# Gated cross-attention block on one core: the pass over the low probabilities last in its unit, auxiliary units in six places instead of three

## What is computed

```python
x = x + tanh(g_xattn[0]) * xattn(layernorm(x), ctx_768, w_q, w_k, w_v, w_o, b_o)
x = x + tanh(g_ffn[0]) * ffn(layernorm(x), ...)

def xattn(x, context, w_q, w_k, w_v, w_o, b_o):        # B=16, Sq=100, Skv=1444
    q, k, v = heads(x @ w_q), heads(context @ w_k), heads(context @ w_v)   # 16 x 64
    attn = softmax(einsum('bhid,bhjd->bhij', q, k) * 64 ** -0.5)
    return merge(einsum('bhij,bhjd->bhid', attn, v)) @ w_o + b_o

def ffn(X, ...):                                        # width 128, 16 heads of 8
    h = rmsnorm(X, norm1_w)
    X = X + self_attention(h @ wq, h @ wk, h @ wv) @ wo
    h2 = rmsnorm(X, norm2_w)
    ...
    return X + shared_swiglu(h2) + top2_experts(h2)
```

## Time and profile before

| | before |
|---|---|
| median of 3 runs | 1532.89 us (1532.3 to 1535.36) |
| the profiled execution | 1536.03 us, span 1534.3 us |
| PE / DVE / ACT / POOL busy | 1374.3 / 1060.1 / 810.3 / 580.3 us |
| mean granted clock of TensorE | 0.965 |
| end of the last score step | about 1365 us; the experts follow |

### The profile page before, as it was taken

One profiled execution on the slowest core, in us unless ns is written; L12 is line 12 of the kernel. 1 busy time (PEld: TensorE's weight loads), 2 busy tenths in 40 slices (PEclk: granted clock), 3 DMA queues, 4 the chain that ended last, 5 costly groups with the idle time before them and its releaser, 6 DMA issues.

```text
span 1534.3 us, 28786 instructions
## 1 busy us (share of the span) xinstructions
PE 1374.3 (90%) x8776; PEld 839.2 (55%) x8776; DVE 1060.1 (69%) x1996; ACT 810.3 (53%) x1188; POOL 580.3 (38%) x702
## 2 busy tenths in 40 slices
PE   4769999999999999999999999899999999888898
PEld 4225555555555565555555555555555555456676
DVE  2777777767676767676767777677767676866665
ACT  1134646555555555555555565556565655554554
POOL 3023334333433434343334333434333433453454
PEclk7579999999999999999999999999999999899999
DMA  7020202020202010010202020202020100000000
GB/s 216 24 56 1 56 1 57 1 58 1 57 1 58 1 32 25 19 39 2 56 2 57 1 57 1 57 1 57 1 58 1 42 1 1 1 1 1 7 7 11
DMA packets 66966, 43.26 MB, mean 28 GB/s; under 512 B 52966, under 2 KB 62410, under 8 KB 66826
## 3 DMA queue, kind: packets, MB, share of 16 engines
q1 hardware_dynamic: 66826, 41.43, 10.7%
HBM read 15.38 MB, written 0.82 MB: 11 GB/s over the span
## 4 chain that ended last, share of the span: by engine, by line
PE 58%; DVE 18%; issue 12%; ACT 4%; POOL 3%; DMA 2%; DVEq 1%; SPq 0%; ACTq 0%; POOLq 0%
PE psum L756 15%; DVE mx L1240 7%; PE psum L816 7%; PE psum L737 6%; PE psum L741 6%; PE psum L739 6%; PE psum L769 4%; PE psum L856 3%; PE psum L808 3%; PE psum L782 3%; PE psum L843 3%; ACT p_hi L952 2%; DVE y_sb L1262 2%; POOL y_sum L575 2%; DVE mx L1274 1%
## 5 line engine op out<-in xcount | busy, mean ns | idle before, releaser
L951 ACT ACTIVATE p<-psum 128x800 f32<-128x800 f32 x384 | 321.1, 836 | 557.2 <-PE psum L741 555.2
L1240 DVE TENSOR_REDUCE mx<-psum 128x1 f32<-128x512 f32 (+1 forms) x624 | 387.6, 654 | 59.2 <-PE psum L816 55.3
L432 POOL TENSOR_TENSOR p_lo<-p,p_hi 128x800 f16<-128x800 f32 x128 | 244.0, 1906 | 482.3 <-ACT p_hi L952 469.3
L756 PE MATMUL psum<-p_hi,c_both 128*128 128x400 f16 x1536 | 390.3, 336 | 26.3 <-POOL p_lo L432 18.0
L952 ACT ACTIVATE p_hi<-psum 128x800 f16<-128x800 f32 x384 | 319.4, 832 | 0.0
L432 DVE TENSOR_TENSOR p_lo<-p,p_hi 128x800 f16<-128x800 f32 x256 | 258.8, 1011 | 54.6 <-issue 20.1
L816 PE MATMUL psum<-cT_both,qk_hi 96*128 96x512 f16 (+1 forms) x624 | 233.2, 388 | 67.3 <-DVE y_sb L1262 19.5
L756 PEld LDWEIGHTS psum<-p_hi,c_both 128*128 128x128 f16 x1536 | 146.7, 98 | 146.0 <-POOL p_lo L432 24.3
L737 PE MATMUL psum<-qk_hi,cT_both 97*128 97x400 f16 x768 | 195.2, 335 | 14.0 <-issue 9.5
L756 PE MATMUL psum<-p_lo,c_both 128*128 128x400 f16 x768 | 194.9, 335 | 0.0
L739 PE MATMUL psum<-qk_lo,cT_both 96*128 96x400 f16 x768 | 194.5, 334 | 0.0
(11 more groups left out here) (183 smaller groups left out, 1774.9 us busy)
## 6 DMA issues: line engine op xcount, KB each, us to landing
c_both<-c_new SPq DMA_DIRECT2D x16, 768.0 KB, 4.0
ctx_nat<-in_ctx_dram SPq DMA_DIRECT2D x16, 528.0 KB
wg<-in_L_ffn_e_gate_dram SPq DMA_DIRECT2D x1, 1024.0 KB, 5.3
wu<-in_L_ffn_e_up_dram SPq DMA_DIRECT2D x1, 1024.0 KB, 7.3
wd<-in_L_ffn_e_down_dram SPq DMA_DIRECT2D x8, 128.0 KB, 4.9
out_dram<-x SPq DMA_DIRECT2D x4, 200.0 KB
x<-in_x_dram SPq DMA_DIRECT2D x1, 600.0 KB
p<-in_L_xattn_w_q_dram SPq DMA_DIRECT2D x1, 512.0 KB, 3.8
```

The source lines that it names most:

```text
L432: engine.tensor_tensor(p_lo[0:m, i % 3, :, :], p32[0:m, i % 3, :, :], p_hi[0:m, i % 3, :, :], ALU.subtract).then_inc(lo_made(b, i)[0], 1)
L756: t = mm(outs[k], w[parity][0:m, j, :], p[0:m, i % 3, k, :], start=(j == 0 and w is c_hi and p is p_hi), stop=(j == CH - 1 and w is c_lo))
L951: a(p32[0:m, i % 3, :, :], src, ACT.Exp, scale=DH ** -0.5)
L1240: v.tensor_reduce(mx[:, rt, part:part + 1], bank[:, 0:w], AX.X, ALU.max)\
```

## The change

In `pv_unit` the pass over `p_lo` moves from second to third place and the wait for it moves in front of that pass. `steps` cuts a step's auxiliary units into sixths, and `score_unit` too now has places for them: behind the first and the second score pass (places 0 and 1), behind the third (2), behind the first and the second value pass (3 and 4), behind the last (5). The cut rounds up: one unit stands in place 0; two in 0 and 3; three in 0, 2 and 4; four in 0, 1, 3 and 4; five in 0 to 4. On DVE, places 0 to 3 come ahead of `p_lo`, 4 and 5 behind. ACT's order is the same as before. A wait for `p_hi` is added before the last two value units, which no score unit precedes.

```diff
-        thirds = [[us[len(us) * k // 3:len(us) * (k + 1) // 3] for k in range(3)] for us in by_place]
-        return thirds, at
+        sixths = [[us[-(-len(us) * k // 6):-(-len(us) * (k + 1) // 6)] for k in range(6)] for us in by_place]
+        return sixths, at
...
-            def score_unit(b, parity, i):
+            def score_unit(b, parity, i, between):
...
                 for k in range(2):
                     mm(outs[k], cT_hi[parity][:, cols], qk_hi[parity][:, qs[k]], start=True, stop=False)
+                between(0)
                 for k in range(2):
                     mm(outs[k], cT_hi[parity][0:C, cols], qk_lo[parity][:, qs[k]], start=False, stop=False)
+                between(1)
                 for k in range(2):
                     t = mm(outs[k], cT_lo[parity][:, cols], qk_hi[parity][0:C, qs[k]], start=False, stop=True)
                 t.then_inc(scores, 1)
...
-                pe.wait_ge(*lo_made(b, i))
                 if i == 0:
                     pe.wait_ge(c_in, (b + 1) * 16)
...
-                for w, p in ((c_hi, p_hi), (c_hi, p_lo), (c_lo, p_hi)):
+                for n, (w, p) in enumerate(((c_hi, p_hi), (c_lo, p_hi), (c_hi, p_lo))):
+                    if p is p_lo:
+                        pe.wait_ge(*lo_made(b, i))
                     for k in range(2):
...
-                    if w is c_hi and p is p_hi:
-                        between()
+                    if n < 2:
+                        between(3 + n)
                 t.then_inc(pv, 1)
...
-                    score_unit(b, parity, i)
-                    one, two, three = steps(kind)[0][i]
-                    run_aux(aux, one, b, kind, parity)
...
+                    score_unit(b, parity, i, between)
+                    between(2)
                     if i >= 2:
-                        pv_unit(b, parity, i - 2, middle)
+                        pv_unit(b, parity, i - 2, between)
...
             for i in (UNITS - 2, UNITS - 1):
+                pe.wait_ge(probs_hi, (B - 1) * UNITS + (i + 1))
                 pv_unit(B - 1, 1, i)
...
-                    one, two, three = steps(kind)[0][i]
-                    run_aux(aux, one, b, kind, parity)
+                    slots = steps(kind)[0][i]
+                    for slot in slots[0:4]:
+                        run_aux(aux, slot, b, kind, parity)
                     if i and i - 1 not in LO_POOL:
                         probs_rest(dve, v, b, i - 1)
```

More of the change, by code:

```diff
@@ L742, in score_unit, with pv_unit @@
                 t.then_inc(scores, 1)
-            def pv_unit(b, parity, i, between=lambda: None):
+            def pv_unit(b, parity, i, between=lambda n: None):
                 j = i % CH
                 m = kc(j)[1]
-                pe.wait_ge(*lo_made(b, i))
                 if i == 0:
@@ L753, in pv_unit @@
                 outs = [psum[:, ACCB + k, 0:GW] for k in range(2)]
-                for w, p in ((c_hi, p_hi), (c_hi, p_lo), (c_lo, p_hi)):
+                for n, (w, p) in enumerate(((c_hi, p_hi), (c_lo, p_hi), (c_hi, p_lo))):
+                    if p is p_lo:
+                        pe.wait_ge(*lo_made(b, i))
                     for k in range(2):
                         t = mm(outs[k], w[parity][0:m, j, :], p[0:m, i % 3, k, :],
-                               start=(j == 0 and w is c_hi and p is p_hi), stop=(j == CH - 1 and w is c_lo))
-                    if w is c_hi and p is p_hi:
-                        between()
+                               start=(j == 0 and n == 0), stop=(j == CH - 1 and p is p_lo))
+                    if n < 2:
+                        between(3 + n)
                 t.then_inc(pv, 1)
@@ L881, in body, with between @@
                 for i in range(UNITS):
-                    score_unit(b, parity, i)
-                    one, two, three = steps(kind)[0][i]
-                    run_aux(aux, one, b, kind, parity)
-                    def middle():
-                        run_aux(aux, two, b, kind, parity)
+                    slots = steps(kind)[0][i]
+                    def between(n):
+                        run_aux(aux, slots[n], b, kind, parity)
+                    score_unit(b, parity, i, between)
+                    between(2)
                     if i >= 2:
-                        pv_unit(b, parity, i - 2, middle)
+                        pv_unit(b, parity, i - 2, between)
                     elif kind != "first":
-                        pv_unit(b - 1, 1 - parity, UNITS - 2 + i, middle)
+                        pv_unit(b - 1, 1 - parity, UNITS - 2 + i, between)
                     else:
-                        middle()
-                    run_aux(aux, three, b, kind, parity)
+                        between(3)
+                        between(4)
+                    between(5)
             batches(pe, body)
             for i in (UNITS - 2, UNITS - 1):
+                pe.wait_ge(probs_hi, (B - 1) * UNITS + (i + 1))
                 pv_unit(B - 1, 1, i)
@@ L1011, in body @@
                         act.wait_ge(scores, b * UNITS)
-                    for third in steps(kind)[0][i]:
-                        run_aux(aux, third, b, kind, parity)
+                    for slot in steps(kind)[0][i]:
+                        run_aux(aux, slot, b, kind, parity)
                     if i == 1 and kind != "first":
@@ L1304, in body @@
                         split_weights(*divmod(i - 4, NW_PARTS))
-                    run_aux(aux, three, b, kind, parity)
+                    for slot in slots[4:]:
+                        run_aux(aux, slot, b, kind, parity)
             batches(dve, body)
```

## The result

The changed kernel takes **1706.35 us** (median of 4 runs, 1703.51 to 1710.34) against 1534.12 us: a ratio of 1.1121, 95% interval 1.1086 to 1.1155. The forecast was 1671 us and its range 1612 to 1703, so the sign held and the size did not: 172 us were lost where 137 were reckoned, and the time lies 3 us outside.

A forecast was written before the change was run, and what follows sets the result against it. TensorE (PE) was taken to set the pace, with short waits. The terms sum to 9.4 us a batch, 132 us over fourteen batches, plus 3 us each for the first and last: 1671 us forecast, range 1612 to 1703.

The forecast's parts named there:

- (a): Step 8: the 1.08 us wait for p_lo goes, but f0 waits for hn, losing 0.68 us; elsewhere worth nothing.
- (b): Steps 12 to 15: p20, p22, p24 and f5 wait for ACT's pT, queued behind the exponentials; +4.4 us a batch.
- (c): Steps 0 to 2: y10 behind the first score pass waits 1.42 us for acc_sb, q2 0.80; +1.7 us a batch.
- (d): Steps 20 and 21: m comes 1.70 us sooner and waits for the row of maxima; +1.5 us a batch.
- (e): Step 17: y_sb of y02 waits for POOL's p_lo, so p28 waits 1.8 us for 0.79; +1.0 us a batch.
- (f): Steps 3 to 8, DVE's: p8 waits 1.1 us, p0 less; +0.4 us a batch with (a) in it.
- the clock: Rival, chance 0.11: waits at y10, p20, p22, m bring clock falls of 1.7 us; 1703 us if one in three.
- The sign that was to point at the clock: The mrow copies, one for each batch, lying over 93 us apart in the profile after; 90.5 us was forecast.

## Why the prediction came out as it did

The steps of a batch, from first score pass to first score pass, as means over fourteen batches: before, after, and after with the 34 added matmuls, where no clock fall is left. The third less the first is what the order costs, the second less the third what the falls cost (4.4 by these means, 4.3 by the copies).

| steps | before, us | after, us | after, no falls, us | order | reckoned | falls |
|---|---|---|---|---|---|---|
| 0 to 2 | 10.1 | 12.0 | 12.0 | +1.9 | +1.7 | 0 |
| 3 to 8 | 18.7 | 18.1 | 18.1 | -0.6 | +0.4 | 0 |
| 9 to 11 | 10.2 | 9.9 | 9.9 | -0.3 | -0.1 | 0 |
| 12 to 15 | 16.9 | 23.8 | 21.8 | +4.9 | +4.4 | +2.0 |
| 16 | 3.6 | 3.9 | 3.7 | +0.1 | +0.2 | +0.2 |
| 17 and 18 | 7.2 | 9.4 | 7.9 | +0.7 | +1.0 | +1.5 |
| 19 | 3.6 | 3.5 | 3.5 | -0.1 | +0.3 | 0 |
| 20 and 21 | 5.0 | 7.3 | 6.7 | +1.7 | +1.5 | +0.6 |
| 22 and 23 | 5.0 | 5.0 | 4.9 | -0.1 | 0 | +0.1 |
| sum | 80.2 | 92.9 | 88.5 | +8.3 | +9.4 | +4.4 |

**(a)**, `p_lo` last: right. In the loop it is worth nothing, and the profile of that part alone shows why with 18.0 us turned into 18.2.

**(b)**, ACT's evacuation: right in mechanism, and 0.5 us too small in size. p20, p22 and f5 wait 1.55, 1.84 and 0.68 us from the modelled end, 1.72, 2.01 and 0.84 from start times, for 1.77, 2.01 and 0.87 reckoned; the four steps cost 4.9 us without a fall, for 4.4.

**(c)** right: y10 waits 1.27 us (1.43 from start times, 1.42 reckoned), q2 0.76 (0.92, for 0.80). **(d)** right on the place; by its own rows it was worth 1.7 us, which is what it cost, though 1.5 went into the sum. `mneg` itself grew (below).

**(e)** p28 waits 1.29 us, 1.46 from start times, for 1.8: over-reckoned by a third of a microsecond. **(f)** had the wrong sign: steps 3 to 8 got faster by 0.6. p8 waited 0.49 us (0.65 from start times) instead of 1.1. The delay of steps 0 to 2 reached DVE, which was idle for 5 of the 10 us of these steps before, only in part; that this is why is argued, not shown. Together the order comes to 8.3 for 9.4.

**What failed** is the treatment of the clock: its falls stood in the sum with nothing, as a rival with a chance of 0.11, and the range's upper end took in only part of that case. The price was somewhat high: 1.7 us for a fall were reckoned, and 4.3 us for the 11.2 us a batch at the lower level are 0.38 for each, 1.3 for a fall of 3.5 us. The count was wrong. With y10, p20, p22 and m as candidates and one in three of them followed by a fall, I had 1.3 falls a batch, 2.3 us; there are 2.7 stretches a batch, some of them two or three times as long, 4.3 us. They follow p24 and p28 too, whose waits I had not counted among them, and never y10. The row behind it was a single fall after 2.16 us of idle time, set against four turns with 1.71 to 1.96 us and none. In the loop before, PE's waits stayed at 0.9 us or less, the turn and one wait of 1.6 us apart, so no row showed several long ones in a batch, and I read waits one by one. In the sum, the 4.3 us are 60 more and the order's 1.1 are 16 less; and outside the loop nothing was lost where 6 us had been reckoned (the copies start 0.6 us later, and the end behind the last copy is 1.9 us shorter). 1671 + 60 - 16 - 7 gives 1708 us. The sign that was to point at the clock, copies over 93 us apart, stayed just silent at 92.8, because the order cost less than reckoned.

The Trainium skill's section on psum-queue depth-cycling (TensorE: Matmul & The Clock Gate), which I set against gaps of under a microsecond, describes what the traces after show: the granted clock swings between its two levels in every batch. That added matmuls stop it is shown by the runs here.

## What to carry to other kernels

Before moving work between two dependent pieces, look at which engine frees what it needs and what is queued ahead of that on this engine: here a 0.5 us copy stood behind two exponentials whose input the move itself delayed, and turning the queue gave back all of the 7.4% that it had cost. A unit that waits for the end of a chain on another engine belongs late in its step, not where the places are evenly spread; but check what the move does to the other engines, as in step 11. Where an edit adds several long waits to TensorE (here six of 1.0 to 1.9 us in a batch), price the clock falls as part of the sum and not as a side case.

## What the runs showed of the hardware

**Added matmuls made the kernel faster.** 476 matmuls that nobody reads, inside waits, raised the mean granted clock from 0.933 to 0.981 and took some 60 us off.

**The length of a wait alone did not decide the fall.** In the fourteen batches y10's wait of 1.27 us was never followed by a fall, p28's of 1.29 us thirteen times and m's of 1.92 us seven times. In the batch shown PE had waited 1.55, 1.84 and 1.03 us in the 22 us ahead of p28, and 1.92 and 0.76 us in the 16 us ahead of y10. What decides is open.

**`mneg` ends when POOL ends.** A DVE instruction with 13 columns from SBUF to SBUF, its duration in ns (shortest, median, longest) in the changed kernel and in the one before:

```profile
L1251 DVE TENSOR_SCALAR mneg<-mx_row x16: 178/1009/1011, 66.4 to 1458.6; 128x13 f16<-128x13 f32 x16
```

```profile
L1246 DVE TENSOR_SCALAR mneg<-mx_row x16: 178/598/1106, 66.5 to 1282.8; 128x13 f16<-128x13 f32 x16
```

At 1270.87 it ran for 1.01 us, to 1271.88; POOL's `p_lo` of step 20 ran from 1270.15 to 1271.85. Before, at 720.08, 0.59 us to 720.67, beside POOL's from 718.94 to 720.64. In every batch of the loop, in both kernels, it ends 0.03 to 0.04 us after POOL's; at 160.20 in the changed kernel, with no POOL instruction beside it, it took 0.18 us. The row of maxima was thus bound to ACT's exponentials of step 20 by way of POOL, in both kernels. The Trainium skill (SBUF — State Buffer, two separate sides) has an exclusive lock on the ports that DVE and GpSimd share, for a DVE instruction with two SBUF inputs or in a two-port mode: the one that starts first holds it to its end. The ends agree with that; `mneg` has one input, and in which mode it ran no row shows. The prediction's reading of that section under (e) was wrong: POOL's `p_lo` at 704.63 met the last 0.57 us of DVE's, not all of it, and its 2.12 us instead of 1.70 agree with waiting that out but for 0.15.

**The turn of the loop** cost PE 1.7 to 2.2 us in five of seven turns before, and almost nothing in the changed kernel (2.5 us in two), where f16 stands at the start of step 23 instead of its end. Putting it back brought the wait back (9.2 us). Why is open.
